# Reordering the ramp of a fused attention kernel on one core: row loads, the first convolution's output, the keys' transfers and the planes of the second image

## The reference

```python
x_ln = layernorm(x, ln_g, ln_b)
q = x_ln @ wq + bq
o = gelu(depthwise_conv7x7_stride2(q) + dw_b)
pos = refs + tanh(conv1x1(o))
interp = bilinear(x, pos)
k = v = interp @ wv + bv
att = softmax((q @ mq_w + mq_b) . (k @ mk_w + mk_b)) (v @ mv_w + mv_b)
z = att @ mo_w + mo_b + x
x = gelu(layernorm(z) @ mlp_w + mlp_b) + z
x = x + sigma * (attention over 2 x 2 max-pooled keys of x)
```

## Time and profile before

| | |
|---|---|
| median of 3 runs | 511.91 us (510.37 to 512.8) |
| the profiled execution: its time | 513.91 us |
| the profiled execution: span of the trace | 512.0 us |
| mean granted clock of TensorE over the span | 0.97 |
| PE busy | 459.8 us (90%) |
| VectorE, ScalarE, GpSimd busy | 56%, 41%, 23% |
| first scores start (end of the ramp) | 73.73 us |

### The profile page before, as it was taken

One profiled execution on the slowest core, in us unless ns is written; L12 is line 12 of the kernel. 1 busy time (PEld: TensorE's weight loads), 2 busy tenths in 40 slices (PEclk: granted clock), 3 DMA queues, 4 the chain that ended last, 5 costly groups with the idle time before them and its releaser, 6 DMA issues.

```text
span 512.0 us, 9321 instructions
## 1 busy us (share of the span) xinstructions
PE 459.8 (90%) x3743; PEld 321.5 (63%) x3743; DVE 285.9 (56%) x609; ACT 212.0 (41%) x338; POOL 120.0 (23%) x163
## 2 busy tenths in 40 slices
PE   7997888987989999989899999989899897988966
PEld 5766655644567576656677665756677574666735
DVE  4628536763773277667853355457536747526343
ACT  1312202643355045654434335745264574462340
POOL 5600201265013001681002003761021030100000
PEclk9998999997999999999999999989999997999989
DMA  7587655674967930393057901473128200000112
GB/s 213 105 159 117 140 86 120 93 186 98 134 92 100 233 47 3 93 115 64 18 121 99 171 3 30 99 100 43 44 64 104 61 24 2 1 2 1 42 42 84
DMA packets 30489, 42.90 MB, mean 84 GB/s; under 512 B 6075, under 2 KB 21230, under 8 KB 30446
## 3 DMA queue, kind: packets, MB, share of 16 engines
q1 hardware_dynamic: 23598, 34.82, 37.1%
q0 software_dynamic: 3584, 4.50, 3.7%
q10 hardware_dynamic: 3264, 2.99, 2.9%
HBM read 16.16 MB, written 4.19 MB: 40 GB/s over the span
## 4 chain that ended last, share of the span: by engine, by line
PE 60%; DVE 13%; DMA 10%; ACT 5%; POOL 5%; issue 5%; ACTq 0%; DVEq 0%; SPq 0%; POOLq 0%
PE ps_d L763 8%; PE ps_d L888 5%; PE ps_d L865 5%; PE ps_d L751 5%; PE ps_d L965 5%; PE ps_s L812 4%; PE ps_v L854 4%; PE ps_v L848 4%; PE ps_t L831 4%; PE ps_d L783 3%; DMA q_st<-mx_t 3%; DVE mx L1615 3%; PE ps_d L907 2%; DMA xa<-in_x_dram 2%; DMA cstack<-att 2%
## 5 line engine op out<-in xcount | busy, mean ns | idle before, releaser
L1230 ACT ACTIVATE prob<-ps_t 128x1024 f32<-128x1024 f32 x64 | 65.4, 1022 | 99.7 <-PE ps_t L831 98.5
L1615 DVE TENSOR_REDUCE mx<-ps_s 128x4 f32<-128x1024 f32 x64 | 78.2, 1221 | 30.4 <-PE ps_s L812 29.5
L1913 POOL DMA_DIRECT2D q_st<-mx_t x64 | 33.9, 532 | 248.1 <-ACT mx_t L1222 230.3
L812 PE MATMUL ps_s<-k_st,q_st 96*128 96x256 f32 x256 | 51.1, 323 | 9.1 <-DVE mx L1615 6.1
L763 PE MATMUL ps_d<-cstack,conv_w 128*32 128x256 f32 x1024 | 59.0, 381 | 0.3 <-issue 0.3
L831 PE MATMUL ps_t<-q_st,k_st 98*128 98x256 f32 x256 | 43.5, 294 | 9.2 <-DMA q_st<-mx_t 4.9
L812 PEld LDWEIGHTS ps_s<-k_st,q_st 96*128 96x128 f32 x256 | 37.0, 196 | 21.6 <-DVE mx L1615 10.4
L763 PEld LDWEIGHTS ps_d<-cstack,conv_w 128*32 128x32 f32 x1024 | 34.6, 108 | 22.4 <-issue 2.9
L831 PEld LDWEIGHTS ps_t<-q_st,k_st 98*128 98x128 f32 x256 | 36.3, 196 | 12.0 <-DMA q_st<-mx_t 5.6
L1629 DVE TENSOR_TENSOR att<-ps_v,rden 128x256 f32<-128x256 f32 x32 | 13.6, 424 | 42.1 <-ACT rden L1241 42.1
L848 PE MATMUL ps_v<-prob,vh 128*32 128x256 f32 x512 | 36.0, 400 | 1.0 <-DVE att L1629 0.9
(11 more groups left out here) (178 smaller groups left out, 756.6 us busy)
## 6 DMA issues: line engine op xcount, KB each, us to landing
q_st<-q_parts SPq DMA_DIRECT2D x42, 256.0 KB, 7.1
xa<-in_x_dram SPq DMA_DIRECT2D x8, 512.0 KB, 6.1
z_all<-in_x_dram SPq DMA_DIRECT2D x8, 512.0 KB, 8.1
out_dram<-z_all SPq DMA_DIRECT2D x8, 512.0 KB, 2.6
cstack<-qpad SPq DMA_DIRECT2D x22, 180.5 KB, 5.7
k_st<-cstack SPq DMA_DIRECT2D x22, 128.0 KB, 4.1
q_st<-z_all SPq DMA_DIRECT2D x6, 256.0 KB, 6.0
cstack<-att SPq DMA_DIRECT2D x6, 180.5 KB, 7.4
```

Source lines behind the costliest of these rows:

```text
L812: ins = pe.matmul(ps_s[:, h, :], q_st[0:96, hg * HQ + h, c0 + half * P:c0 + (half + 1) * P], k_st[0:96, b % 2, h, hg, :], start=True, stop ...
L1230: drain(act.activation(prob[:, u % 2, 2 * pr:2 * pr + 2].rearrange("p h m s -> p (h m) s"), ps_t[:], ACT.Exp), t_ring, "t", b, u, pr)
L1615: drain(dve.tensor_reduce(mx[:, u % 2, half, :], ps_s[:], AX.X, ALU.max), s_ring, "s", b, u, half)
```

## The change

In words:

- SP loads image 1's rows as soon as the planes of the first half (cb 0) have landed, no longer behind those of the second half; the stacking of the queries stays behind the second half's.
- VectorE reads the first convolution (`conv_out(0, 0)`) ahead of the scaling of image 1's rows (`row_scale(1)`), behind their statistics.
- PE makes the second head group of `queries(0, 1)` behind the keys; the order of the banks follows.
- ScalarE makes the keys' high parts ahead of the queries' and issues one key DMA, for head group 0; VectorE forms both samples, the keys' low parts and the values' bias ahead of the queries' low parts.
- SP issues head group 1's key rows, now all three, when group 0's three have landed.
- SP stacks image 1's planes of half 1 only when the corners of the second samples have landed.
- The output weights are loaded behind image 2's rows, no longer in slot 3.

```diff
--- before.py
+++ after.py
@@ -129,8 +129,8 @@
 
     order = [("qimg", 0, cb, jp) for jp in range(2) for cb in range(CB)]
     order += [("qh", 0, 0, hg) for hg in range(NHG)] + [("conv", 0, cb) for cb in range(CB)] + [("off", 0)]
-    order += [("qimg", 1, 1, jp) for jp in range(2)] + [("qimg", 1, 0, 0), ("qh", 0, 1, 0), ("qh", 0, 1, 1)]
-    order += [("kh", 0), ("qimg", 1, 0, 1), ("conv", 1, conv_halves(1)[0])]
+    order += [("qimg", 1, 1, jp) for jp in range(2)] + [("qimg", 1, 0, 0), ("qh", 0, 1, 0), ("kh", 0)]
+    order += [("qh", 0, 1, 1), ("qimg", 1, 0, 1), ("conv", 1, conv_halves(1)[0])]
     for b, s in slots():
         n, m, mm = b + 1, b - 1, b - 2
         cur, post, fin = b < B, 0 <= m < B, 0 <= mm < B
@@ -582,8 +582,11 @@
                             sp.wait_ge(k_lo_done.sem, k_lo_done.at(b, 1))
                         else:
                             sp.wait_ge(k.drained, k.done)
-                        if b == 0 and row == 1:
+                        if b == 0 and hg == 0 and row == 1:
                             continue
+                        if b == 0 and hg == 1 and row == 0:
+
+                            sp.wait_ge(k_in[0].sem, k_in[0].at(0, 3))
                         sp.dma_start(k_st[32 * row:32 * row + 32, b % 2, :, hg, :].bitcast(F32),
                                      k_parts[:, part, hg, :].bitcast(F32)).then_inc(k_in[hg].sem, 16)
 
@@ -614,7 +617,6 @@
                     if s == 3:
                         behind_max_row(b, 3)
                         load_z(b)
-                        for_output.start(sp)
                     if s == 5:
                         behind_max_row(b, 5)
                 if s == 2 and 1 <= b < B - 1:
@@ -647,15 +649,19 @@
             stack_conv(0, 0)
             stack_conv(0, 1)
 
+            sp.wait_ge(conv_in[0].sem, conv_in[0].at(0, 4))
+            load_a(1)
             sp.wait_ge(conv_in[1].sem, conv_in[1].at(0, 4))
-            load_a(1)
             stack_q(0, 0, [0])
             stack_q(0, 0, [1])
+
+            sp.wait_ge(corners_in[1].sem, corners_in[1].at(0, 2))
             stack_conv(1, 1)
             stack_k(0)
             stack_conv(1, 0)
             behind_max_row(0, 0)
             load_a(2)
+            for_output.start(sp)
             behind_max_row(0, 1)
             stack_q(0, 1, [0])
             for b, s in slots():
@@ -1085,9 +1091,10 @@
             q_image(1, 1)
             q_image(1, 0, [0])
             setup_values()
-            queries(0, 1)
+            queries(0, 1, [0])
             pe.wait_ge(setup_act, A_ALL)
             keys(0)
+            queries(0, 1, [1])
             q_image(1, 0, [1])
             conv(1, conv_halves(1)[0], STEPS_OF_1[0])
 
@@ -1416,13 +1423,12 @@
             conv_gelu(0, 1)
             offset_tanh(0)
             setup_values()
-            query_hi(0, 1)
             act.wait_ge(setup_dve, D_BIAS)
             key_hi(0)
-            for hg in range(NHG):
-                act.wait_ge(k_hi_done.sem, k_hi_done.at(0, hg + 1))
-                act.dma_start(k_st[32:64, 0, :, hg, :].bitcast(F32), k_parts[:, 0, hg, :].bitcast(F32)
-                              ).then_inc(k_in[hg].sem, 16)
+            act.wait_ge(k_hi_done.sem, k_hi_done.at(0, 1))
+            act.dma_start(k_st[32:64, 0, :, 0, :].bitcast(F32), k_parts[:, 0, 0, :].bitcast(F32)
+                          ).then_inc(k_in[0].sem, 16)
+            query_hi(0, 1)
             for b, s in slots():
                 slot(b, s)
             tail(B - 1)
@@ -1877,8 +1883,8 @@
             query_lo(0, 0)
             bias_row_parts(mlpb_hl, mlpb_all, BIAS_EMPTY)
             row_stats(1)
+            conv_out(0, 0)
             row_scale(1, range(NT))
-            conv_out(0, 0)
             row_shift(1, range(NT))
             setup_key_bias()
             for_q.wait(dve)
@@ -1887,12 +1893,11 @@
             q_image(1, 1)
             q_image(1, 0, [0])
             sampled(0, 0)
-            query_lo(0, 1, [0])
             sampled(0, 1)
-            query_lo(0, 1, [1])
             dve.wait_ge(setup_dve, D_BIAS)
             key_lo(0)
             setup_values()
+            query_lo(0, 1)
             q_image(1, 0, [1])
             for b, s in slots():
                 slot(b, s)
```

## The result

The changed kernel took 510.25 us (median of 21 runs, 507.6 to 512.75) against 512.96 for the kernel before (21 runs, 509.48 to 517.72): ratio 0.9948, with a 95% interval of 0.9928 to 0.9969. That is 2.7 us, where 7.2 were forecast (504.7 against the 511.91 of three runs), and 510.25 lies outside the stated range of 501.3 to 509.5. The profiled execution's span is 508.4 us.

What follows compares the result with a forecast made beforehand. With PE busy 90% of the span, gains had to come from its waits in the ramp. 5.9 (scores) + 1.35 (clock) + 0.7 (weights) - 0.7 (image 2) = 7.25, giving 504.7 us against 511.91; range 501.3 to 509.5.

Steps and rivals of the forecast that it cites:

- The rows' landing: Ramp: image 1's second half, loaded earlier by SP, lands at 36.7 instead of 39.96, 3.2 us earlier.
- no gain: Ramp: the latest landing allowed for image 1's rows, 39.96, as in the kernel before.
- The first rival: Ramp: image 1's rows' load gains nothing; keys at 60.4, scores at 70.9, total 507.8; chance 0.17.
- The prediction's own sign of being wrong: End of the ramp: wrong if scores start after 71, or a wait on planes stands before the second planes' convolution.
- Image 2's rows and the first maximum row: Slots behind the ramp: traffic makes image 2's load, VectorE's statistics and the maxima late; loss 0.7 us, bounds 0 and 1.5.
- K: Start of the keys on PE: 64.26 in the kernel before, forecast at 57.3, a gain of 7.0 us.
- K to S: From the keys' start to the first scores' start on PE: forecast 10.5 us, 1.0 more than before.
- the clock's fall: Behind the first scores: the lower clock level from 73.7 to 82.0 goes with PE's wait; gain 1.35, bounds 0 and 1.7.
- The last corner: Image 0's last gather transfer, with planes held back: takes 3.9 us instead of 7.6, landing at 55.0 instead of 62.0.
- Output weights: Three loads moved from slot 3 to slot 1, easing a maximum row's transfer; gain 0.7 us, between 0 and 1.3.
- The second: Rival: image 1's second planes take 10.1 us instead of 5.4 and land 3.0 late; total 507.7, chance 0.10.
- The third rival: New waits before keys and image part lower the clock, and later stretches shift: 5.1 us, total 509.9; chance 0.09.

Runs made afterwards that it cites:

- e6: Changed kernel with the queries' six transfers issued only when image 1's rows have landed; 506.89 us, ratio 0.9876.
- e9: Changed kernel with queries' transfers held behind image 1's rows and head group 1's key rows not waiting for group 0's landing; 504.39 us, ratio 0.9827.
- e12: e9 with image 1's rows loaded behind both halves' planes again; 505.49 us, ratio 0.9842.
- e3: Changed kernel without the wait of head group 1's key rows for group 0's landing; 508.29 us, ratio 0.9874.
- e2: Changed kernel with the output weights' three loads back in slot 3; 510.64 us, ratio 0.9935.
- e8: Changed kernel with image 2's rows loaded right behind the second planes, without waiting for the first maximum row; 511.00 us, ratio 0.9961.
- e1: Changed kernel with image 1's rows loaded behind both halves' planes again; 507.51 us, ratio 0.9886.
- e11: e6 with VectorE's read of the first convolution put back behind the scaling of image 1's rows; 507.07 us, ratio 0.9872.
- e5: Changed kernel with image 1's rows at their old place and head group 1's key rows not waiting for group 0; 507.85 us, ratio 0.9897.
- e7: Kernel before, with only image 1's planes of half 1 held until the last corner has landed; 511.28 us, ratio 0.9963.
- e4: Changed kernel with image 1's planes of half 1 no longer held behind the corners; 512.59 us, ratio 0.9960.
- e10: e9 with image 2's rows loaded behind the keys and ahead of the second planes; 504.95 us, ratio 0.9827.

## Why the prediction was wrong

**The rows' landing, 36.7, bounds 33.5 to 39.96: failed.** It was 40.8, outside both bounds. I saw that the load would move behind SP's planes, and about 37.9 is where it lands when nothing follows (e6, e9). I left out that the queue behind it moved up with it: the six transfers of queries, in all 1.5 MB, were issued at 34.62 and are now at 33.36, when the rows' packets are just leaving. The upper bound "no gain" took for granted that an earlier issue can't land later. The first rival names these transfers, and I spoke against it with "they idle after", of the DMA engines behind 33.6. That is wrong: their share is 0.47 from 33.6 to 36, and they are then full up to 46, at the end of it with the queries. Windows of the kernel before, columns as in the earlier trace rows:

```profile
42.00:46.00 4.00, 1.87 (x22) 1.19 (x14) 3.96 (x11) 2.03 (x4) 0.00 (x0) 1.00 1.07 173
```

The same of the changed kernel, then of e6:

```profile
33.00:36.00 3.00, 3.00 (x58) 1.95 (x54) 0.00 (x0) 0.00 (x0) 0.00 (x0) 1.00 1.10 343
36.00:38.00 2.00, 2.00 (x43) 1.42 (x37) 1.41 (x4) 0.00 (x0) 0.00 (x0) 1.00 1.09 131
```

```profile
33.00:36.00 3.00, 3.00 (x58) 1.92 (x54) 0.00 (x0) 0.00 (x0) 0.00 (x0) 1.00 1.05 307
36.00:38.00 2.00, 2.00 (x44) 1.22 (x36) 1.46 (x5) 0.00 (x0) 0.00 (x0) 1.00 0.13 30
```

Nearly all of the rows moves between 33 and 36 in both (343 and 307 GB/s). What is late is a tail. Of the rows' 1024 packets 24 end behind 36.2 in the changed kernel, the last at 39.04; in e6 34 do, the last at 37.44, while the engines stand almost empty (0.13). So the queries' transfers stretch the last few packets by 1.6 us, and what follows them to the landing by 1.2.

In the Trainium skill, "DMA: Bandwidth & Descriptors", section "Queues, rings and completion order", each engine takes a queue's descriptors in ring order, and a later one may finish its write before an earlier one. e9 beside e12 agrees with the ring order (5.2 us of earlier issue, 0.7 of landing), though mere contention would look the same; and the order of the descriptors did not keep the rows from being held up by 2.8 us by transfers behind them.

The step cost 4.1 us at the landing: 2.8 by the queries' transfers, and 1.2 because a landing 4 us behind the plane was too early a figure even without them. It was 3.9 at the gather (51.03 for 47.1) and 4.1 at keys and scores. The prediction's own sign of being wrong, scores after 71, was there: 71.89.

**Image 2's rows and the first maximum row, 0.7 with bounds 0 to 1.5: mis-sized.** It measured 2.8: a lead of 3.3 at the first unit's maxima, 0.5 at gather 1. I had them meet the second planes and counted 2 us of lateness in the load. I had put those planes at 70, which is K + 12.7, and they were issued at 74.09, which is again K + 12.7: the length of the two groups' turns was right, and the planes are 4.1 late because the keys are. Two other things were off. The load, issued 3.26 us behind the first unit's maxima in the kernel before (82.92 - 79.66), is issued 5.67 behind them here (82.04 - 76.37), so 2.4 later against PE and not 2. And its two DMAs then took 5.3 and 6.4 us where I had left them at 3.5 and 4.5, 1.9 more. Of these 4.3 us the 1.1 that VectorE had to spare come off, which leaves 3.2, and it waits 3.03. I had put the statistics at 1.4 late and passed half of that on; nearly all of the 3.0 reached gather 1. e3 and e9 show that the turn-taking brings both; e2 that it isn't the weights' traffic; e8 that it isn't the wait for the maximum row by itself. What makes the load itself slower is not shown. The traces split by one thing: in the five in which both DMAs took 5.3 to 7.4 us (changed, e1, e2, e6, e11) one instruction packet of 16 KB (queue 8) starts amid the rows' packets, in the changed kernel from 84.49 to 85.45, and in those in which both took 3.3 to 4.8 (before, e3, e5, e7, e9, e12) none does before the rows are nearly or wholly through. In e4 it starts between the two landings, and only the second is late (3.4 and 5.9); e8 and e10 load amid planes or keys. No run moved that packet alone.

**What held.** K to S was forecast at 10.5, 1.0 more than before, with a wait of 1.3 before the image part: it is 10.51, with 1.27. The keys' rows beat PE's work, the wait for them is gone, and in this execution the clock's fall behind it too (1.35 forecast; from 1.8 at the scores the lead rose to 3.3, so 1.5). That the one follows from the other isn't shown, and e7 speaks against it (the same wait, no fall); the size is in part luck. The last corner took 4.3 against the 3.9 taken for it. The exchange of read and scaling is worth nothing through the positions (e11). Output weights: 0.7 forecast, none seen (e2), though its interval doesn't exclude 0.7. The positions come 8.8 us behind the rows' landing (49.57 - 40.8), for 8.9. With the queries held the forecast's gather, keys and scores all came within 1.1 us (e6), and with the turn-taking gone too the forecast's 504.7 was measured as 504.4, by a kernel that isn't the changed one. That they agree so closely is luck: beside that kernel the one before took 514.29, not the 511.91 that the forecast starts from, and the ratio is 0.983 where the forecast's was 0.986.

**The rivals.** The first ("the rows' load gains nothing", keys 60.4, scores 70.9, 507.8) is nearest to what happened in the ramp, each 1 us optimistic. The second saw late planes but looked for the cost in their own convolution, where PE never waited; it was VectorE, behind planes, maximum row and load, that stood. They happened together, and I had priced them as alternatives: 507.8 and the 2.1 us lost in slot 2 beyond the 0.7 make 509.9, against 510.25 measured. This too closes better than it should: both are counted from 511.91, and from the 512.96 measured now the same sum gives 511.0. The third rival's price was added up wrongly by 0.1 (504.7 + 5.1 = 509.8), which changes nothing.

## What to carry to other kernels

When a DMA issue is moved up, everything behind it on that queue moves up too: work out what these transfers will meet, before the one that was moved. An earlier issue can land later, so "no gain" is no bound. And when a ramp gets shorter, ask of each load with a late start whether it starts earlier as well; here one held transfer and one removed wait (e9) were worth over twice the change itself.

## What the runs showed of the hardware

Two DMAs of 4 KB, issued by GpSimd, took 1.6 us to land when the planes were through (before, from 80.75), 4.0 among 722 KB of planes (changed), and 7.0 with 1 MB of rows and the output weights added (e8): here a small transfer paid for what another queue, SP's, had in flight. PE stood 1.64 us inside image 0's second convolution with nothing to wait for ("issue", at 42.3). The same wait, 1.28 to 1.80 us at the same place, is in each of the five traces in which the rows are early and the queries not held (changed, e2, e3, e4, e8), and in none of the nine others. The DMA queues from 40 to 43 have this line in the changed kernel, and its like in the four other traces with the wait:

```profile
q8 instruction: 1, 0.02, 3.3%
```

In the nine without the wait no packet of queue 8 starts in that window. In the five it ends at 42.0 to 42.6, and PE goes on 1.6 to 1.8 us later; in the others the packet of that stage had ended by 40.9. So it looks as if PE's instructions were late behind the data, though no run moved them alone, and it isn't shown. The granted clock fell to the lower level over the image products in all eleven traces in which PE had waited between the convolutions and them by 0.7 us (e11) to 3.0 us (e7) in all; in e6, e9 and e10, with 0.36 to 0.47, it stayed at the upper one.
